# Three groups of products and one norm moved between the slots of a software-pipelined two-layer kernel

## The reference, cut to what matters

```python
xn = layernorm(x)                                  # 4 sequences x 1024 tokens x 128 features
s  = retention(xn)                                 # (q k^T * decay) v
h  = silu(xn w1^T) * (xn w2^T)                     # 128 -> 512
h  = gelu(h h1^T); h = gelu(h h2^T)                # 512 -> 512, twice (exact gelu)
x  = x + s * silu(h w3^T)                          # 512 -> 128
xn = layernorm(x)
xc = silu(causal_conv4(xn W_in)); B, C = xc W_x
state = A * state + xc * B; y = C . state + D * xc # scan over the tokens, 128 x 16 states
s  = (y * silu(gate)) W_out
w  = sigmoid(score), kept for the 512 best of 1024 tokens of a sequence
u  = w * (gelu_tanh(xn W1 + b1) W2 + b2)           # the update, 128 -> 512 -> 128
x  = x + s * silu(xn + u)
```

## Time and profile before

| | |
|---|---|
| three timed executions | 632.33, 637.34, 638.47 us; median 637.34 us |
| the profiled execution | 640.04 us, of which 638.3 us lie between its first and last instruction |
| PE busy | 496.8 us (78%), 1875 matmuls |
| DVE busy | 488.8 us (77%) |
| POOL busy | 350.5 us (55%) |
| ACT busy | 292.8 us (46%) |
| mean granted PE clock | 0.915 of full speed |
| ACT_TABLE_LOAD, whole program | 27 |

### The profile page before, as it was taken

The page is one execution under the profiler, slowest core; times in us unless marked ns, Lnnn a source line. Parts: engine busy times, 40 slices in busy tenths (PEclk is TensorE's granted clock), DMA queues, the critical chain, the costliest instruction groups (busy, mean ns, idle before and its releaser), DMA issues.

```text
span 638.3 us, 6072 instructions
## 1 busy us (share of the span) xinstructions
PE 496.8 (78%) x1875; PEld 280.8 (44%) x1875; DVE 488.8 (77%) x749; ACT 292.8 (46%) x467; POOL 350.5 (55%) x346
## 2 busy tenths in 40 slices
PE   1328869986998789978998799968987898685762
PEld 0215635643564446534654356434643464331220
DVE  2542042897589978996799968997899869969894
ACT  3315564644563646443745455445734553422200
POOL 1705442868384548655663738565855485533232
PEclk9999898997999989996998799989999898886985
DMA  8200000000000000000000000001000000000000
GB/s 327 108 2 1 1 17 1 2 16 0 2 1 17 0 33 1 16 1 33 3 0 17 1 33 0 0 2 34 1 0 1 16 2 1 0 17 1 0 17 16
DMA packets 5650, 11.82 MB, mean 19 GB/s; under 512 B 880, under 2 KB 1520, under 8 KB 5360
## 3 DMA queue, kind: packets, MB, share of 16 engines
q1 hardware_dynamic: 4464, 9.47, 4.1%
q10 hardware_dynamic: 1152, 1.93, 0.9%
HBM read 9.30 MB, written 2.10 MB: 18 GB/s over the span
## 4 chain that ended last, share of the span: by engine, by line
DVE 40%; PE 30%; issue 12%; ACT 10%; POOL 6%; DMA 1%; DVEq 0%; SPq 0%; POOLq 0%; ACTq 0%
PE bank0a L822 9%; DVE xbank L1201 7%; PE bank1a L893 6%; DVE hs L1213 6%; DVE beats L1178 4%; DVE beats L1167 4%; PE ybank L953 4%; DVE beats L1176 3%; DVE tie L1171 3%; DVE beats L1174 2%; PE bank1a L878 2%; POOL hs L479 2%; DVE plain L1102 2%; ACT yn L605 1%; ACT L557 1%
## 5 line engine op out<-in xcount | busy, mean ns | idle before, releaser
L479 POOL TENSOR_TENSOR hs<-hs,Ct 128x512 f32<-128x512 f32 x128 | 167.0, 1305 | 92.3 <-DVE hs L1213 86.8
L942 PE MATMUL xbank<-xpair,spr 128*128 128x512 f32 x128 | 76.3, 596 | 55.0 <-DVE hs L1213 54.8
L1201 DVE TENSOR_TENSOR xbank<-xbank,Bt 128x512 f32<-128x512 f32 x128 | 87.9, 687 | 35.2 <-PE xbank L942 35.1
L465 POOL TENSOR_TENSOR hidAl<-plain,hidAh 128x512 fp32r<-128x512 f32 x48 | 62.7, 1306 | 61.1 <-ACT hidAh L558 40.0
L557 ACT ACTIVATE plain<-bank0a,col 128x512 f32<-128x512 f32 x64 | 44.1, 689 | 95.3 <-PE bank0a L822 94.2
L465 POOL TENSOR_TENSOR hidBl<-plain,hidBh 128x512 fp32r<-128x512 f32 x48 | 62.2, 1296 | 45.8 <-ACT hidBh L558 33.6
L1213 DVE TENSOR_TENSOR_SCAN hs<-decay,carry,xbank 128x512 f32<-128x512 f32 x64 | 81.8, 1278 | 7.0
L1213 DVE TENSOR_TENSOR_SCAN hs<-decay,xbank 128x512 f32<-128x512 f32 x64 | 78.0, 1218 | 4.7
L942 PEld LDWEIGHTS xbank<-xpair,spr 128*128 128x128 f32 x128 | 25.7, 201 | 105.7 <-DVE hs L1213 90.1
L822 PE MATMUL bank0a<-hidAh,hTh 128*128 128x512 f32 x128 | 56.7, 443 | 4.7 <-ACT hidBh L558 3.4
L822 PE MATMUL bank0a<-hidBh,hTh 128*128 128x512 f32 x128 | 57.9, 452 | 2.1 <-ACT hidAh L558 1.9
(11 more groups left out here) (155 smaller groups left out, 1032.4 us busy)
## 6 DMA issues: line engine op xcount, KB each, us to landing
xt<-x_tok SPq DMA_DIRECT2D x8, 256.0 KB, 2.6
xr<-x_feat SPq DMA_DIRECT2D x8, 256.0 KB, 8.2
out<-xr SPq DMA_DIRECT2D x8, 256.0 KB, 2.0
fh<-h_w SPq DMA_DIRECT2D x1, 1024.0 KB, 10.7
hs<-h_w SPq DMA_DIRECT2D x1, 1024.0 KB, 13.0
lw<-l_w ACTq DMA_DIRECT2D x1, 640.0 KB, 7.0
g<-spread ACTq DMA_DIRECT2D x1, 512.0 KB, 6.2
Bt<-w_in SPq DMA_DIRECT2D x1, 512.0 KB, 8.4
```

The costliest lines, as they stand in the source:

```text
L465: pool.tensor_tensor(low[:, m, :], plain[:, k % NPLAIN, :], high[:, m, :].bitcast(F32), ALU.subtract).then_inc(hidden_low, 1)
L479: pool.tensor_tensor(h, h, Ct[:, hs_(u)], ALU.mult).then_inc(p_ready, 1)
L942: pe.matmul(xbank[i % 2][:], spr[:, at, :], xpair[:, half, hs_(u)], start=True, stop=True).then_inc(xs_full, 1)
L1201: dve.tensor_tensor(xbank[i % 2][:], xbank[i % 2][:], Bt[:, hs_(u)], ALU.mult).then_inc(xb_ready, 1)
```

## The change

The memory sums of unit v go from slot 9 to slot 2 on PE, between the first and the second product of the slot's z pair, and `take_u` on ACT to the end of slot 2, behind the second layer's norm. The four up products of the update go from slots 14 and 15 of their own period to slot 9 of the next, where the memory sums were; ACT takes them there, behind the first layer's norm. The last unit's (unit 7) stay where they were. The first layer's norm goes one slot ahead on ACT (8), two on POOL (6) and two on DVE (5).

```diff
@@ the order of the bank jobs
     if _v is not None:
-        L0_ACT += [("z1", _v, 2), ("z1", _v, 3)] + [("h1", _v, _m) for _m in range(KT)] + [("u", _v), ("h2", _v, 0)]
+        L0_ACT += [("z1", _v, 2), ("u", _v), ("z1", _v, 3)] + [("h1", _v, _m) for _m in range(KT)]
+    if _t is not None and _t != UNITS - 1:
+        L0_ACT += [("ffn", _t, _m) for _m in range(KT)]
+    if _v is not None:
+        L0_ACT.append(("h2", _v, 0))
...
-    if _n is not None:
+    if _n == UNITS - 1:
         L0_ACT += [("ffn", _n, _m) for _m in range(KT)]
@@ GpSimd
-                if w is not None and s == 8:
+                if w is not None and s == 6:
                     rstd_l0(w)
@@ ScalarE
-                if w is not None and s == 9:
+                if w is not None and s == 8:
                     norm_l0(w)
-                if v is not None:
-                    if s == 9:
-                        take_u(v)
...
+                if v is not None and s == 2:
+                    take_u(v)
+                if t is not None and t != UNITS - 1 and s == 9:
+                    for m in range(KT):
+                        mod_up(t, m)
@@ TensorE
+                    if v is not None and s == 2:
+                        retention_out(v)
                     if v is not None and s < KT:
                         z2(v, s)
...
-                    if v is not None and s == 9:
-                        retention_out(v)
+                    if t is not None and t != UNITS - 1 and s == 9:
+                        for m in range(KT):
+                            mod_up(t, m)
...
-                    if n is not None and s >= 14:
+                    if n == UNITS - 1 and s >= 14:
                         mod_up(n, 2 * (s - 14))
                         mod_up(n, 2 * (s - 14) + 1)
@@ VectorE
-                    if s == 7:
+                    if s == 5:
                         stats_l0(w)
```

More of the change, by code:

```diff
@@ L702, in slot @@
                             sigmoid_half(n // 2)
-                if w is not None and s == 9:
+                if w is not None and s == 8:
                     norm_l0(w)
-                if v is not None:
-                    if s == 9:
-                        take_u(v)
-                    if 10 <= s < 10 + KT:
-                        hidden("h2", v, s - 10)
+                if v is not None and s == 2:
[3 more added lines that the diff above has]
+                        mod_up(t, m)
+                if v is not None and 10 <= s < 10 + KT:
+                    hidden("h2", v, s - 10)
                 if w is not None:
@@ L714, in slot @@
                         retention_q(w)
-                if n is not None:
-                    if s == 14:
-                        mod_up(n, 0)
-                        mod_up(n, 1)
-                    elif s == 15:
-                        mod_up(n, 2)
-                        mod_up(n, 3)
+                if n == UNITS - 1 and s >= 14:
+                    mod_up(n, 2 * (s - 14))
+                    mod_up(n, 2 * (s - 14) + 1)
                 if t is not None and t >= UNITS - 2 and s == update_slot(t) + 1:
```

## The result

The changed kernel takes 667.64 us (median of four executions, 665.48 to 668.66), the kernel before 637.0 in the four executions beside it. The ratio is 1.049, with a 95% interval of 1.044 to 1.054: slower by 4.9%. The prediction had said 655 us with a range of 642 to 669, and slower with 0.80. So the direction and the range held, and the size was 13 us short.

What follows compares the result with a forecast made beforehand. DVE was taken to bound slot 9 to slot 3 of the next period, PE slots 4 to 8. Sum: 640.04 + 18.3 + 3.5 - 5 + 1 = 657.8 us, carried over to the median 655; range 642 to 669.

Steps and rivals of the forecast that it cites:

- rival C: Slower still: delayed POOL work lengthens DVE's comparisons, 9 us, with upper-end waits and no clock gain; 673 us, chance 0.13.
- Up products in slot 9: ACT comes late and loads tables twice, so PE and then DVE wait: 18.3 us over six periods.
- Up products out of slots 14 and 15: Taking them off PE there gains nothing, since they lie beside DVE's work, which is late next.
- rival B: Faster: PE is the bound, so slot 15 gives back up products' time and the clock stays up; 619 us, chance 0.07.
- Memory sums in slot 2: ACT's `take_u` lengthens the hand-over to PE's gather by 0.5 us in each of seven periods, 3.5 us.
- The clock in slots 3 to 5: The sums fill PE's gap, so its clock may stay up: bounds 0 and -9.7 us, taken as -5.
- Norm earlier: Moving the first layer's norm on DVE, POOL and ACT costs nothing, within 0.3 us either way a period.
- Start: In period -1 nothing hides the sums in the z chain: +2.5 us, about 1.5 back in slots 9 and 10: +1.
- The table load's drain: The skill's 1.38 us of drain per ACT table switch would add 8.3 us, giving 663; given no chance of its own.

Runs made afterwards that it cites:

- e4: e1 with `take_u` one slot later, behind the second z bank of slot 3; 638.93 us, ratio 1.003 against the kernel before.
- e1: The changed kernel with the up products put back into slots 14 and 15; 643.51 us, ratio 1.010 against the kernel before.
- e6: The kernel before with only the first layer's norm moved earlier; 632.73 us, ratio 0.998.
- e10: The kernel before with one more wait: POOL starts its last three start operations only after DVE has made `w3l`; 634.69 us, ratio 1.001.
- e7: The kernel before with PE's gather of slot 4 put behind the convolution; 625.56 us, ratio 0.987.
- e8: e4 and e7 together, up products in slots 14 and 15; 624.27 us, ratio 0.985 against the kernel before.
- e9: The kernel before with POOL's weighing multiplying only 8 of 512 columns, so the output is another one; 584.59 us, one execution.
- e5: The changed kernel with ACT taking the up products ahead of the sigmoids and the norm; 652.81 us, ratio 1.024 against the kernel before.
- e3: The changed kernel with the update's tanh gelu replaced by exact gelu (another function), 20 table loads for 32; 650.11 us, ratio 1.019 against before.

## Why the prediction was right in direction and short in size

The measured 667.6 us lie 12.6 above the forecast, 1.4 below the upper end of the range, and nearer to rival C (673, chance 0.13) than to the forecast. Of C's parts the longer comparisons came (5.4 of its 9 us) and the missing clock gain, but not the upper ends of all waits. The range held because it reached into C.

**"Up products in slot 9": right, and the main term.** 18.3 us foretold, 19.6 measured. The rows came as described: a load, four gelus, a second load that waits for PE, PE idle 4.23 us in odd periods (4.1 foretold) and 2.18 in the even ones 2 and 4, the spread late by 3.29 in period 3 (2.0 to 3.6 foretold), the ranking products late. The chain of an odd period came at its upper end: from the gate's `Bt` to the end of the ranking products 18.8 us in period 3, where the steps with the low clock give 18.7 (334.6 less 315.94). I had taken 4.0 of those 4.5 us; the hold was 4.7 in periods 3 and 5 and 5.7 in period 1. Even periods were to be 2.1, 3 at most, and came at 2.4 and 4.0; their lower bound of 1.5 had no working behind it. What sets the periods apart is the clock behind PE's new wait. Mean granted clock from 4 to 12 us behind the gate's `Bt`: 0.57, 0.79 and 0.79 in periods 1, 3 and 5, and 1.00 and 0.79 in periods 2 and 4. Period 6 was valued like an even one and came out at -2.0. There is no unit 8, so ACT has no norm there and is free in time; that could have been read from `units`, where w is none. That it is less than nothing comes from two comparisons, which took 1.49 and 1.35 us before and 0.48 and 0.35 after.

**"Up products out of slots 14 and 15. I value it at nothing": right.** DVE had no idle time there before, and PE's wait for the scan only grew: 2.11 us in the earlier trace rows, now

```profile
353.00 0.50 PE L944 MATMUL xbank<-xpair,spr 128*128 128x512 f32 x1 [2.70 <-DVE hs L1218]
```

This is rival B's refutation: the chain of waits had passed through PE there, and taking 1.9 us of PE's work away gave nothing. In period 3 both kernels take 20.9 us from the scan behind `token_weights` to the statistics.

**"Memory sums in slot 2", 0.5 us in each of seven periods: right in kind.** +2.6 measured against 3.5. But by period the stage goes from -0.4 to +1.4, since the gather's own 1.07 or 1.93 us lie in it; what shows the copy's part is the 0.46 us a period of e4. That the sums' going from slot 9 is worth nothing did not hold in e1: +2.8 us (e6).

**"The clock in slots 3 to 5 ... I take the middle, -5": failed,** one of the two largest misses. In the prediction's own measure, from the gather to the next spread over periods 1 to 6, it was 37.1 us before and is 38.2 after: 1.0 longer, not 5 shorter. The sums did fill PE's gap: 2.48 us of idle time in the earlier trace rows became 0.73. But the wait ahead of the gather grew from 1.44 to 2.21 us. Timeline of PE in the kernel after, slots 3 and 4 of period 4:

```profile
369.36 0.50 PE L944 MATMUL xbank<-xpair,spr 128*128 128x512 f32 x1 [0.73 <-DVE hs L1218]
...
374.73 1.85 PE L955 MATMUL ybank<-hs,gat 128*32 128x512 f32 x8 [2.21 <-POOL hs L483]
```

The mean granted clock of the 8 us around the first convolution product, read from the windows of each kernel, period by period:

| kernel | periods 1 to 7 | mean |
|---|---|---|
| before | 0.50 0.64 0.60 0.50 0.90 0.87 0.60 | 0.66 |
| e10 (PE's order as before) | 0.66 0.89 0.96 0.93 0.63 0.88 0.60 | 0.79 |
| after | 1.00 0.79 0.57 0.79 0.60 0.79 0.74 | 0.75 |
| e1 (`take_u` in slot 2) | 0.57 0.57 0.57 1.00 0.79 0.79 0.57 | 0.69 |
| e4 (`take_u` in slot 3) | 1.00 1.00 0.79 1.00 0.79 1.00 0.63 | 0.89 |
| e7 (gather behind, gap of 2.48 us kept) | 0.59 0.57 0.82 0.58 0.81 0.59 0.50 | 0.64 |
| e8 (both) | 1.00 1.00 0.79 1.00 0.80 1.00 0.52 | 0.87 |

These are one profiled execution each, and e10 says how little one can bear: its PE has the order and the gap of the kernel before, and stands at 0.79. It takes 30.8 us from gather to next spread over the six periods, as little as e4 (30.7), while e6, with the same slots 2 to 4, takes 37.1 like the kernel before. So 6.3 of the 9.7 us that the prediction set down for the filled gap come and go between executions with the gap left as it is.

Steadier is the mean granted clock of whole executions, which was taken for each one. Its median is 0.917 to 0.922 for the kernel before in the three groups of comparisons, 0.924 in e1, 0.927 after and 0.939 in e4. In e7 it is 0.920 to 0.922 and in e8 0.941 to 0.952, four executions each: there the clock goes up with the sums in the gap, and not by the norm's move, since e6 stays at 0.921. It gave no time that these runs can tell (625.56 and 624.27 us). That in the changed kernel `take_u` stood in the way of it, by lengthening the wait behind the gap, is supported by e1 against e4, one edit apart, and not shown: e4's own executions go from 0.913 to 0.946. Either way the term was not independent of its neighbour.

The Trainium skill's rule (TensorE: Matmul & The Clock Gate, HAM oscillation), read as I had read it, gives the whole 9.7 us for the filled gap. The trace of after doesn't bear that out. The waits of the page's own example are longer than the 2.48 us here. For the new wait of slot 9 the reading fits better: behind 4.23 us of idle time the clock fell in all three odd periods, behind 2.18 us in one of two.

**The other largest miss, a term that was not in the sum: token weights to statistics, +5.4 us.** Rival C had it ("the delay pushes POOL's work beside DVE's comparisons"), at 1.5 us a period, and it came at 1.4 in each odd period and 0.2 to 0.7 in the others. The rows above show the whole of it in period 3: from L1189 (339.81) to the scan at 345.63 it is 5.82 us, and in the kernel before it was 4.43, from 330.08 to this scan:

```profile
334.51 1.26 DVE L1213 TENSOR_TENSOR_SCAN hs<-decay,carry,xbank 128x512 f32<-128x512 f32 x1
```

Of the 1.4 us, 1.0 is the comparison at 343.15, which takes 1.36 us where its counterpart in the earlier trace rows, at 333.05, took 0.34. Another 0.3 is the one at 340.42, 1.33 us where it was 0.99. POOL meanwhile runs this:

```profile
340.31 1.29 POOL L469 TENSOR_TENSOR hidAl<-plain,hidAh 128x512 fp32r<-128x512 f32 x1
341.55 1.33 POOL L483 TENSOR_TENSOR hs<-hs,Ct 128x512 f32<-128x512 f32 x1
343.00 1.36 POOL L469 TENSOR_TENSOR hidAl<-plain,hidAh 128x512 fp32r<-128x512 f32 x1
```

e9 shows that POOL's operations are what makes comparisons long. That the one at 343.00 costs the 1.0 us is read from the rows. No kernel moved it alone, but in e5, where it falls otherwise, the same comparison takes 0.34.

**"Norm earlier. Nothing": right** (e6). **"Start, +1": small and near,** -0.2 from the first z product to the statistics of period 1. Ahead of it the profiled execution of after is 3.8 us shorter, for a reason that has nothing to do with the change (last section). Against the medians instead of these two profiles the change costs 30.6 us, 5 more than the spans say.

**The table load's drain.** In the fence of ACT above, the load at 325.12 starts where the norm's row ends (324.38 and 0.72 us), and the gelus start where the load ends. Twelve loads fewer gave 17.5 us, 1.46 each, and each row is 1.28. The rule (the Trainium skill, ScalarE: Activation LUTs, What ACT_TABLE_LOAD costs) adds some 1.38 us to each load. An estimate by that page, 12 times 2.66 us, would have made e3 about 32 us faster; the trace doesn't show that. The page's advice to batch calls by table (its section Table sets) was right for this change all the same.

## What to carry to other kernels

Before work is moved into a "free" slot, look at the engine that takes it up: PE had room in slot 9, but ACT changed its table twice there and came late, and two banks turned both into waits of PE. Of several waits on one path only the last releaser's lateness against its slack counts, and two terms that meet in one place (the filled gap, and the copy that lengthened the wait behind it) have to be valued together. Before the low clock of a stretch is given a price, see whether another execution of the same kernel has it too. If PE waits for another engine ahead of work that doesn't depend on it, try the other order first: gather behind convolution gave 1.3%.

## What was unexpected of the hardware

**A small operation of DVE stands until POOL's operation ends.** In the kernel before, L1178 (128x128, 32 times) takes 1.35 to 1.38 us in the 18 rows that start less than 0.2 us behind the start of a POOL operation, and 0.34 us in the 14 others, beside which POOL does nothing. It looks like all or nothing because DVE and POOL start together there. The line ahead of it, L1171, meets POOL's operations at any point: it takes 0.32 to 0.34 us in 16 rows, and in the 16 others 0.56 to 1.26 us, which is each time 0.14 to 0.16 us more than what was left of POOL's operation. With POOL's weighing cut to 8 columns (e9) the mean of the 32 falls from 0.917 to 0.440 us. The Trainium skill (SBUF — State Buffer, Who interferes with whom) describes it as a lock on a pair of ports, where the second to come blocks for the whole operation of the first; these rows agree.

**DVE can stand through several operations of POOL in a row.** At the start, DVE's `w3l` is a 512-column subtraction. In the kernel before it took

```profile
25.46 6.18 DVE L1290 TENSOR_TENSOR w3l<-Ct,w3h 128x512 fp32r<-128x512 f32 x1
```

beside four of POOL's (timeline of POOL in the kernel before):

```profile
22.84 4.59 POOL L508 TENSOR_TENSOR hTl<-hs,hTh 128x2048 fp32r<-128x2048 f32 x1
27.40 1.25 POOL L447 TENSOR_TENSOR xnTl<-xnT,xnTh 128x512 fp32r<-128x512 f32 x1
28.62 1.25 POOL L454 TENSOR_TENSOR q<-q,grow 128x512 f32<-128x512 f32 x1
29.84 1.25 POOL L513 TENSOR_TENSOR w_conv<-lw,gate 128x512 f32<-128x512 f32 x1
```

and it ended 0.55 us behind the last. In the changed kernel it got in behind the first, and POOL's next was the one that stood:

```profile
25.76 2.46 DVE L1295 TENSOR_TENSOR w3l<-Ct,w3h 128x512 fp32r<-128x512 f32 x1
```
```profile
23.15 4.52 POOL L512 TENSOR_TENSOR hTl<-hs,hTh 128x2048 fp32r<-128x2048 f32 x1
27.64 1.71 POOL L451 TENSOR_TENSOR xnTl<-xnT,xnTh 128x512 fp32r<-128x512 f32 x1
```

Of the profiled executions of before, after and e1 to e9, six have the short form (2.42 to 2.47 us), with the first z product at 37.9 to 38.8 us, and five the long one (6.14 to 6.19), with it at 42.0 to 42.9. Neither goes with the change. The long form stood in the profile of before and the short one in that of after, which is the -3.8 in the table of stages: two single profiles can differ at their start by more than an edit is worth, so compare them stage by stage.
